# A Mamba layer with routed experts: expert weights loaded in pieces beside the main loop, the first slot table made earlier, routed steps begun one iteration sooner

## What is computed

```python
x = layernorm(x + mamba(x))
gates = softmax(x @ router_w)                     # 14 routed experts, the best two are kept
h_e = x * rsqrt(mean(x*x) + eps) * rms_w[e]       # per expert
ffn_e = silu(h_e @ w1[e]) @ w2[e]
x = layernorm(x + sum_top2(gate_e * ffn_e) + ffn_s0 + ffn_s1)
```

## Time and profile before

| | us |
|---|---|
| three runs | 744.18, 745.13, 746.52 |
| median | 745.13 |
| profiled execution, its own time | 745.25 |
| its span, first to last instruction | 743.5 |
| PE, DVE, POOL, ACT busy | 629.1, 594.7, 511.8, 444.3 |
| mean granted TensorE clock | 0.951 |

### The profile page before, as it was taken

One profiled execution on the slowest core, in us unless ns is written; L12 is line 12 of the kernel. 1 busy time (PEld: TensorE's weight loads), 2 busy tenths in 40 slices (PEclk: granted clock), 3 DMA queues, 4 the chain that ended last, 5 costly groups with the idle time before them and its releaser, 6 DMA issues.

```text
span 743.5 us, 14720 instructions
## 1 busy us (share of the span) xinstructions
PE 629.1 (85%) x4299; PEld 533.4 (72%) x4299; DVE 594.7 (80%) x1745; ACT 444.3 (60%) x1225; POOL 511.8 (69%) x559
## 2 busy tenths in 40 slices
PE   5987788999999999999999999799987888767700
PEld 4676567777877877878878788688887788657600
DVE  4999979999999999999999989655826544567736
ACT  4885687687687687687787776263313122344727
POOL 1144455688778778777778787747777777788862
PEclk9999999999999999999999999899999999989855
DMA  8641111112122212211212210913423333665317
GB/s 316 200 130 41 30 58 38 51 58 64 51 59 63 55 58 59 57 54 55 62 54 58 61 33 28 307 43 81 118 81 107 94 108 101 193 197 155 109 54 267
DMA packets 62639, 70.76 MB, mean 95 GB/s; under 512 B 10335, under 2 KB 45285, under 8 KB 62304
## 3 DMA queue, kind: packets, MB, share of 16 engines
q1 hardware_dynamic: 52656, 52.79, 24.9%
q0 software_dynamic: 8608, 16.87, 6.6%
q10 hardware_dynamic: 1296, 0.16, 0.1%
HBM read 48.55 MB, written 23.01 MB: 96 GB/s over the span
## 4 chain that ended last, share of the span: by engine, by line
PE 35%; issue 15%; POOL 15%; ACT 13%; DVE 7%; DMA 2%; SPq 1%; POOLq 0%; DVEq 0%; ACTq 0%
POOL returned L589 11%; PE bank L850 5%; PE bank L792 5%; PE bank L783 4%; ACT x L899 4%; ACT rows L991 2%; PE bank L837 2%; PE bank L847 2%; PE bank L766 2%; PE bank L799 2%; PE bank L751 2%; POOL dispatched L648 2%; PE bank L854 2%; PE bank L758 2%; PE bank L814 2%
## 5 line engine op out<-in xcount | busy, mean ns | idle before, releaser
L589 POOL DMA_INDIRECT returned<-xT,slots_in x141 | 142.9, 1014 | 44.1 <-issue 41.8
L648 POOL DMA_INDIRECT dispatched<-rows,row_u x128 | 149.6, 1169 | 31.7 <-issue 31.6
L1107 DVE SCALAR_TENSOR_TENSOR xbcT_area<-raw,conv_w,xbcT_area 128x512 f32<-128x512 f32 x162 | 125.7, 777 | 3.2 <-ACT xbcT_area L965 3.2
L910 ACT ACTIVATE raw<-bank 128x512 f32<-128x512 f32 (+1 forms) x71 | 40.7, 589 | 85.7 <-PE bank L718 82.5
L718 PE MATMUL bank<-xT 128*128 128x128 f32 x564 | 75.6, 290 | 17.6 <-DVE xT L1377 16.8
L936 ACT ACTIVATE zs<-bank 128x256 f32<-128x256 f32 x64 | 24.2, 379 | 110.2 <-PE bank L751 110.2
L1115 DVE TENSOR_TENSOR_SCAN decay_area<-decay_area,ident_heads 128x512 f32<-128x512 f32 x64 | 86.9, 1358 | 0.0
L718 PEld LDWEIGHTS bank<-xT 128*128 128x128 f32 x564 | 70.8, 203 | 20.0 <-DVE xT L1377 17.1
L1388 DVE COPY xT<-bank 128x512 f32<-128x512 f32 (+1 forms) x36 | 24.4, 677 | 65.4 <-DMA returned<-xT,slots_in 51.6
L738 PE MATMUL bank<-xbcT_area,raw 128*128 x564 | 72.9, 286 | 0.8 <-ACT raw L910 0.7
L899 ACT ACTIVATE x<-x,shift,rstd 128x128 f32<-128x128 f32 x128 | 52.1, 480 | 35.0 <-DVE shift L1098 35.0
(11 more groups left out here) (225 smaller groups left out, 1516.4 us busy)
## 6 DMA issues: line engine op xcount, KB each, us to landing
decay_area<-decay_rows SPq DMA_DIRECT2D x64, 256.0 KB, 3.3
slots_in<-dispatched SPq DMA_DIRECT2D x141, 64.5 KB, 2.1
hid<-returned SPq DMA_DIRECT2D x18, 256.0 KB, 3.6
xT<-xT_dram SPq DMA_DIRECT2D x8, 512.0 KB, 8.3
x<-x_dram SPq DMA_DIRECT2D x8, 512.0 KB, 7.7
out_dram<-x SPq DMA_DIRECT2D x16, 256.0 KB, 4.8
xT<-returned SPq DMA_DIRECT2D x14, 256.0 KB, 3.8
returned<-xT,slots_in POOLq DMA_INDIRECT x141
```

What stands on the lines that cost most here:

```text
L589: e.indirect_dma_start(returned, bass.IndirectOffsetOnAxis(ap=slots_in[sb_][:, n, D:ROW].bitcast(U32), axis=0), slots_out[b][:, n * P:(n + ...
L648: e.indirect_dma_start(dispatched, bass.IndirectOffsetOnAxis(ap=row_u[t % 2][:, m:m + 1], axis=0), rows[t % 3][:, k, c4, :], None).then_in ...
L1107: e.scalar_tensor_tensor(o, r[:, n:n + W], conv_w[:, k, TAPS - 1 - n:TAPS - n], o, ALU.mult, ALU.add).then_inc(S["conv"])
```

## The change

Five things are changed together.

1. `w1_routed` moves to the front of `xT` (columns of tiles 0 to 6, free once their shared hidden units are done) and is loaded by SP in seven pieces of two experts, 256 KB each, behind the decay loads of chunks 24, 28 ... 48, each behind a wait for `hidden`.
2. ScalarE scales each piece by `rms_w` four iterations later (iterations 28 to 52); the 14 DVE instructions of iteration 66 are gone.
3. The early table is made in iterations 50 to 58, three instructions at the end of each iteration, with its scratch in `decay_turned`. SP can so load groups 0 to 2 before the loop ends.
4. `w2_routed` moves to the decay buffers and is loaded ahead of group 3, after the last `mix`.
5. `ROUTED_AT` is now [65, 66, 67, 69, 71, 73, 75, 77, 78 to 83]: each step n >= 2 comes one entry sooner (the first `down` in iteration 67, not 69), 12 groups in the loop instead of 11. `pick_w1(0)` moves to step 0. Ring buffers of the routed steps are placed anew.

```diff
...
@@ -111,8 +111,13 @@
     LAST_A, LAST_M = (((TOP_K * n * 4 * P + NR * (P - 1)) // P - 1) // 4 for n in (NA, NM))
-    ROUTED_AT = [NC + 2, *range(NC + 3, NC + 13, 2), *range(NC + 13, LAST)]
+    ROUTED_AT = [NC + 1, NC + 2, *range(NC + 3, NC + 14, 2), *range(NC + 14, LAST)]
     FILL_AT = EARLY_GROUPS - 2
+
+
+    W1_AT = [4 * (n + 1) + LAG + 4 for n in range(NR // 2)]
+    W1_SCALED_AT = [c + 4 for c in W1_AT]
+    TABLE_FROM = 4 * NA + 18
     TAIL_FROM = LAST_A + 5
     TAIL_BESIDE = min(NM, GROUPS - TAIL_FROM)
@@ -254,7 +259,10 @@
         decay_area = sb("decay_area", [P, 7, NH, P])
         decay_all = [decay_area[:, i] for i in range(5)]
         running = [decay_area[:, 5 + i] for i in range(2)]
-        w1_routed = decay_area[:].rearrange("p n h i -> p (n h i)")[:, 0:NR * HB * P].rearrange("p (e f) -> p e f", e=NR)
+
+        w1_routed = xT[:, 0:NR * HB * P].rearrange("p (e f) -> p e f", e=NR)
+        assert 2 * HB * P == W
+        w2_routed = decay_area[:].rearrange("p n h i -> p (n h i)")[:, 0:NR * HB * D].rearrange("p (e f) -> p e f", e=NR)
         raw = sb("raw", [P, NBLK, TAPS - 1 + W])
         xbcT_area = sb("xbcT_area", [P, 2, NBLK, W])
         x_third = sb("x_third", [P, DI // P, W])
@@ -264,7 +272,6 @@
             if k < DI // P:
                 return x_third[:, k] if t % 3 == 2 else xbcT_area[:, t % 3, k]
             return xbcT_area[:, t % 2, k]
-        w2_routed = xbcT_area[:].rearrange("p n k i -> p (n k i)")[:, 0:NR * HB * D].rearrange("p (e f) -> p e f", e=NR)
         zs = [sb(f"zs{i}", [P, DI]) for i in range(3)]
         bt = [sb(f"bt{i}", [P, P]) for i in range(3)]
         mix = [sb(f"mix{i}", [P, NH, P]) for i in range(2)]
@@ -320,11 +327,14 @@
             return carve, at
         slots_in = [sb(f"slots_in{i}", [P, 4, ROW]) for i in range(7)]
         carve, used = carver(xT[:])
+        carve(NR * HB * P)
+        w1_now = [carve(HB * P) for _ in range(8)]
+        slotsT = [carve(W)]
+        AREA_UNITS = 4 * -(-used[0] // W)
+        carve, _ = carver(xbcT_area[:].rearrange("p n k i -> p (n k i)"))
+        slotsT += [carve(W) for _ in range(2)]
         slots_out = [carve(W) for _ in range(3)]
-        slotsT = [carve(W) for _ in range(3)]
-        w1_now = [carve(HB * P) for _ in range(8)]
         gexp = carve(NC * NR).rearrange("p (c r) -> p c r", c=NC)
-        AREA_UNITS = 4 * -(-used[0] // W)
         carve, _ = carver(raw[:].rearrange("p k i -> p (k i)"))
         hidden_r = [carve(W) for _ in range(4)]
...
@@ -453,6 +463,10 @@
                 on.wait_ge("running", c + 1 - len(decay_all))
                 src = decay_rows[c * NH:(c + 1) * NH, :].unsqueeze(0).to_broadcast([P, NH, P])
                 e.dma_start(decay_all[b], src).then_inc(S[f"decay{b}_loaded"], 16)
+                if c in W1_AT:
+                    n = W1_AT.index(c)
+                    on.wait_ge("hidden", 4 * (n + 1))
+                    e.dma_start(w1_routed[:, 2 * n:2 * n + 2], w1_v[:, 2 * n:2 * n + 2]).then_inc(S[f"w1r{n}_loaded"], 16)
 
             def pick(m):
@@ -477,12 +491,8 @@
             on.wait_ge("dispatched1", NA // 2 * 8 * 16)
             on.wait_ge("early_table", EARLY_ROWS)
             for gr in range(GROUPS):
-
-                if gr == 1:
+                if gr == 3:
                     on.wait_ge("mix", NC)
-                    e.dma_start(w1_routed, w1_v[:, 0:NR]).then_inc(S["w1r_loaded"], 16)
-                if gr == 2:
-                    on.wait_ge("y_out", NC)
                     e.dma_start(w2_routed, w2_d[:, 0:NR * HB * D].rearrange("p (e f) -> p e f", e=NR)).then_inc(S["w2r_loaded"], 16)
                 if gr == FILL_AT:
@@ -900,7 +910,8 @@
             def routed_silu(gr):
-                on.wait_ge("early_table", EARLY_STEPS)
+                on.wait_ge("conv", 3 * NT * NBLK)
+                on.wait_ge("halo", 2 * NT)
                 for n2 in pairs_of(gr):
                     on.wait_ge("routed_hidden", n2 + 1)
                     was = n2 - len(hidden_r)
@@ -997,6 +1008,12 @@
                     on.wait_ge("xnT", t + 1)
                     on.wait_ge("z", 4 * t + 4)
                     e.activation(xnT[t], act_ring.bank("xnT", t)[:], ACT.Copy).then_inc(S["xnT_copied"])
+                if i in W1_SCALED_AT:
+                    n = W1_SCALED_AT.index(i)
+                    on.wait_ge(f"w1r{n}_loaded", 16)
+                    on.wait_ge("rms_w_loaded", 16)
+                    for r in (2 * n, 2 * n + 1):
+                        e.activation(w1_routed[:, r], w1_routed[:, r], ACT.Copy, scale=rms_w[:, r:r + 1]).then_inc(S["w1r_scaled"])
                 n = routed_step(i)
                 if n is not None and n >= 1:
                     routed_silu(n - 1)
@@ -1223,8 +1240,7 @@
                 of8 = tile_no[0:TPE, :].unsqueeze(2).to_broadcast([TPE, 8, NR])
                 by_tile = lambda a: a[0:TPE, :].unsqueeze(1).to_broadcast([TPE, 8, NR])
-                on.wait_ge("conv", 3 * NT * NBLK)
-                on.wait_ge("halo", 2 * NT)
+                on.wait_ge("decay_rows", 16 * len(TURNS))
                 on.wait_ge("early_total", 1)
                 step(e.scalar_tensor_tensor(rows_a, expert_no, -float(REGION), total_a[:], ALU.mult, ALU.add))
                 yield
@@ -1359,6 +1375,9 @@
             def turned(gr):
                 on.wait_ge("slotsT", gr + 1)
+                if gr:
+
+                    on.wait_ge("y_out", NC)
                 if gr >= len(slotsT):
                     on.wait_ge("routed_hidden", 2 * (gr - len(slotsT)) + 2)
                 cols = slice(0, len(slot_tiles(gr)) * P)
@@ -1369,7 +1388,7 @@
             def pick_w1(gr):
                 if gr % 2 == 0:
                     experts[:] = experts_of(on, ET.DVE, gr)
-                on.wait_ge("w1_scaled", NE)
+                on.wait_ge("w1r_scaled", NR)
                 for n in slot_tiles(gr):
                     was = n - len(w1_now)
                     if was >= 0:
@@ -1445,8 +1464,8 @@
                 if i in STEPS_FROM:
                     later = steps_of(STEPS_FROM[i])
                     next(later)
-                if i == NC - 2:
-                    later = early_table()
+                if i == TABLE_FROM:
+                    first_table = early_table()
                 if i == 0:
                     on.wait_ge("w_out_loaded", 16)
                     on.wait_ge("norm_w_loaded", 16)
@@ -1492,18 +1511,19 @@
                         on.wait_ge("down", 4 * t + 4)
                         on.wait_ge("x1", 4 * t + 4)
                         e.tensor_tensor(x[:, 4 * t:4 * t + 4, :], down_bank[:].rearrange("p (c d) -> p c d", c=4), x[:, 4 * t:4 * t + 4, :], ALU.add).then_inc(S["shared_added"])
-                if i == NC + 2:
-                    run(later)
-                    on.wait_ge("w1r_loaded", 16)
-                    for n in range(NR):
-                        e.tensor_scalar(w1_routed[:, n], w1_routed[:, n], rms_w[:, n:n + 1], None, ALU.mult).then_inc(S["w1_scaled"])
+                if TABLE_FROM <= i < NC - 4:
+                    for _ in range(-(-EARLY_STEPS // (NC - 4 - TABLE_FROM))):
+                        next(first_table, None)
                 n = routed_step(i)
+                if n == 0:
+                    on.wait_ge("hidden", AREA_UNITS)
+                    pick_w1(0)
                 if n == 1:
                     on.wait_ge("hidden", AREA_UNITS)
                     for gr in range(2):
                         turned(gr)
-                        pick_w1(gr)
+                    pick_w1(1)
                 elif n is not None and n >= 2:
                     routed_group(n - 2)
 
```

More of the change, by code:

```diff
@@ L37 @@
     "rate", "dt_exp", "chunk_decays", "step_decay", "rows_copied", "xbc_raw", "xbc_silu", "z_silu", "xdt", "g_squares", "bt",
-    "gT_copied", "x1", "x2", "xn", "xnT_copied", "hidden_silu", "routed_silu", "gate_exp", "second_scaled",
+    "gT_copied", "x1", "x2", "xn", "xnT_copied", "hidden_silu", "routed_silu", "gate_exp", "second_scaled", "w1r_scaled",
     "dt_raw", "chunk_sums", "rows_turned", "xbc", "z", "token_major", "gram", "state_add", "y_out", "gT",
@@ L348, in mamba_moe @@
         seg_row, seg_len = (sb(n, [P, 3, NR]) for n in ("seg_row", "seg_len"))
-        carve, _ = carver(raw[:].rearrange("p k i -> p (k i)"))
+        carve, _ = carver(decay_turned[:].rearrange("p n i -> p (n i)"))
         lower_a = carve(NR * NR).rearrange("p (a b) -> p a b", a=NR)
@@ L373, in mamba_moe @@
             [f"{n}_loaded" for n, _, _ in small_params] + [f"xT{b}_loaded" for b in range(NB)]
-            + [f"x{b}_loaded" for b in range(NB)] + ["w_in_loaded", "w1_loaded", "w2_loaded", "w1r_loaded", "w2r_loaded",
+            + [f"x{b}_loaded" for b in range(NB)] + ["w_in_loaded", "w1_loaded", "w2_loaded", "w2r_loaded", *(f"w1r{n}_loaded" for n in range(NR // 2)),
                "filler_region", "filled", "dispatched0", "dispatched1", "stored", "decay_rows"]
```

## The result

The changed kernel takes **746.8 us** (median of 18 runs, 745.4 to 748.6), the kernel before 744.3 (18 runs on the same chips, 741.7 to 746.5). The ratio is 1.0034 with a 95% interval of [1.0025, 1.0043]: some 2.5 us slower, just beyond the 0.3% that the prediction gave as the least that can be told from no change, and 0.6 us from its 746.2. That closeness is kinder than the forecast earned: it added 1.1 us to a median of 745.1 for the kernel before, and what was measured is 2.5 us on one of 744.3. The profiled executions are 1.4 us apart (745.25 and 746.67; spans 743.5 and 744.9); the rest is that the profiled run of before lay 0.9 above its own median.

The account below looks back on a forecast made before the run. PE and DVE were taken to bound the main loop, POOL's queue the end from 496 us. 745.25 us profiled + 4.0 (loop) - 2.9 (transition) = 746.35, less 0.12 to the median: 746.2 us; range 741.0 to 750.0.

Parts of the forecast that it names:

- the base: Time of the kernel before, where the sum starts: 745.25 us for the profiled execution, 745.1 as median of runs.
- By then PE has paid it all: +4.0 us.: Loop, by iteration 59: the table's instructions on DVE make `mix` late and PE waits for it; +4.0 us.
- Scaling on ScalarE, cost 0.: Loop, iterations 28 to 52: 14 activations of some 0.4 us each, covered by ACT's 2.03 us wait for PE; 0.
- Transition, -2.9 us.: From iteration 66 to POOL's first returns: first return 11.8 us sooner, of which POOL keeps -2.9 us.
- The idle time is exchanged, not removed.: POOL, transition: the early return stands ahead of iteration 68's work, so POOL idles 8.7 us before it.
- From there POOL is full again: POOL, from the second return, ready at 496.9 us: no more waiting for data; no cost in the sum.
- Later: Tail: group 12's reload is covered by four groups of returns, not five; costed at nothing, else a us or two.
- Rival 1: Loop: room behind `mix` and DVE's waits absorb nearly all of the table, 0.5 us left; 742.7 us, chance 0.17.
- Rival 2: Transition: PE is the bound and all its 6.8 us come back; 742.3 us, chance 0.13.
- The other reading: Transition: occupancy names PE as the engine to work on, its 6.8 us loss is recovered whole; 742.3 us.
- Rival 3: POOL, iteration 67: a late first `down` makes the early return block POOL for nothing; 749.1 us, 0.28 with the w2 rival.
- Rival 4: Transition: w2 lands after 481 us and PE stands again; 8 us of margin, chance 0.28 with the blocked-POOL rival.

Follow-up runs that it names:

- pieces_alone: Changed kernel with routed steps at their old iterations and the table made from iteration 62, run out at 66, as before; 739.9 us, ratio 0.9941 to before.
- steps_as_before: Changed kernel with the routed steps at their old iterations (from 66 on); 741.5 us, ratio 0.9972 to the kernel before.

## Why the prediction was right, and where it was not

The three parts, by the ratios of kernels taken one part at a time: pieces, scaling and what goes with them **-4.4 us** (before to pieces_alone), the table in 50 to 58 **+2.3** (to steps_as_before), the early routed steps **+4.6** (to the changed kernel), each by the intervals good to some 1.5 to 2 us. That they add up to +2.5 says nothing by itself, since each starts where the last one ends; and a part's price hangs on what it is added to: the table costs 1.5 us in the kernel before, its interval 0.5 to 2.5.

The prediction had the order of events and came within 0.6 us of the time, the latter in part by luck. By the profiled runs the loop costs 2.5 and not 4.0, the tail 1.8 and not 0; the two errors nearly cancel, and the base, too high by 0.8, did the rest.

1. *"By then PE has paid it all: +4.0 us."* Right in kind, mis-sized: +2.5 from mark to z, in all four kernels of the table of runs that have the slot table there, and 0 to -0.4 in those without. PE's waits on `mix` rose by 3.3 us (0.3 to 3.6), near the predicted 4, but its waits on ScalarE's `zs` fell by 0.9, which the sum had left out.
2. *Scaling on ScalarE, cost 0.* Right. The 14 activations take 0.56 us each where 0.4 was reckoned from z's, 0.95 for a pair, with 1.24 us of ScalarE's wait still left behind them, and the loop of pieces_alone is as long as before (311.2).
3. *Transition, -2.9 us.* Right to 0.1: from the mark the last z is 2.5 later, the set 0.4 earlier. So are its steps: from z to the first return 25.4 us were reckoned and 25.3 measured; an idle stretch of 8.7 was reckoned and is 9.2; g_rs, the dispatches, DVE's residual and rstd follow in the reckoned order.
4. *"The idle time is exchanged, not removed."* Right, and shown: the return one iteration later, or the routed steps at their old iterations, each with the loop as long as in the changed kernel, end the set 4.2 us sooner (353.2 to 349.1). The first of the two moves nothing but POOL's queue. The prediction saw what stood behind the return and still took the transition as one term, so it never asked what the early steps were worth by themselves, a loss of 4.6 us.
5. *"From there POOL is full again"*, *Later* costed at nothing. Full it is, no return of the tail waits over 0.3 us for data, but not at the same pace: 1.8 us were lost from the set to the last return. This is the weakest step. It took 1.30 us for a return as fixed; two returns took 0.7 us more, and one gap 0.66. Why those two are long and what the gap is stays open; that returns slow down beside VectorE's copies is shown, but by 0.03 to 0.15 us each.

Rival 1 (the loop absorbs the table) had its place right and its size wrong: 1.5 of the 4.0 were absorbed, not 3.5. Rival 2 (all of PE's loss comes back) fell in this kernel, whose PE is busy at full clock while nothing is won; it is near to what pieces_alone shows, where the set comes 6.9 us sooner from the mark and the time falls by 4.4. The other reading set beside the sum, 742.3, was not borne out for the change as a whole. The Trainium skill (Perfetto Trace Analysis, Identifying the Most-Contended Engine) would in fact not have led to PE by its 85%: it takes matmul busy time for no good measure of TensorE and goes by the weight loads, here 72%, less than DVE's 80%. Rival 3's mechanism, a return that blocks POOL, was at work without its condition: the first `down` came as early as reckoned and the order still cost 4.2 us. Rival 4: w2 had landed.

## What to carry to other kernels

On an in-order queue that is the bound, starting a producer's work sooner helps only if what is ready does not stand behind it: list the queue's entries with the time at which each could run, and issue in that order. Price each part of a change against the kernel without that part; a right total can hold a gain and a loss of 4 us each. Where a saturated loop must take more vector work, put it where the loop's own work has thinned out, here the four iterations behind the last convolution: the last z matmul then comes as early as in the kernel before (310.8 to 311.2 us from the mark, against 313.7).

## What had not been expected of the hardware

POOL's indirect DMAs and VectorE's copies from SBUF to SBUF slow each other, by a little. In the twelve profiles at least 146 returns begin within 0.45 us of the start of a burst of four float32 copies of 128x256. Of these 146, 138 take 0.97 to 1.10 us, most of them 1.03 to 1.10, against a usual 0.97. Where the return takes only 0.97, in about half of the cases the burst is the one that is longer, 1.09 to 1.32 us in place of 0.89. With three times the columns copied, 17 of 28 returns are delayed so, in place of 5 to 7; with the copies on ScalarE, 2.

The other eight take 1.64 to 1.69 us. They are the same two returns, near 532 and 534 us in the changed kernel, in four kernels. The Trainium skill (SBUF — State Buffer, "SBUF: two separate sides") says that a float32 copy on VectorE holds the port which the GpSimd cores need to write a transfer's descriptors, and that the loser waits until it ends. The trace agrees in kind: either side can be the one that waits, and the usual delay is less than one copy of the burst (0.89 / 4 = 0.22 us). It does not explain the two long returns: held through the whole burst, they would be 0.77 and 0.84 us longer, where 0.67 and 0.72 is measured, but the 138 others had up to 1.1 us of their burst ahead of them too and were not held through it.

The spread of a kernel's runs, some 3 to 5 us, has at least one source ahead of the mark: profiled runs of kernels with the same instructions there reach the mark at 146.7 to 149.8 us, and run alike behind it. What makes that difference was not looked into.
